# Loading both top-2 expert weights per visit instead of keeping all eight experts on chip

## The chip, the cores and the metric

The kernel runs on one core of one Trainium2 chip. The core has five engines that run side by side: TensorE (PE, matmuls), VectorE (DVE), ScalarE (ACT), GpSimd (POOL) and SyncE (SP, which here only issues DMAs). They meet only at semaphores. The metric is device time in microseconds (us), lower is better, given as the median of several runs.

## The reference

The input is `x`, 16 sequences of 256 tokens with 256 features. Four blocks are added to it one after the other: an mLSTM-like attention, an expert layer of 16 experts with fixed capacity, a causal linear attention, and a top-2 expert layer with a layer norm at its end. The change touches the last one. Cut to what matters (T = 4096 tokens, D = 256, H = 1024, E = 8):

```python
logits = x @ Wg + bg                          # T x 8
top2_vals, top2_idx = top_k(logits, 2)
scores = softmax(top2_vals)
h = gelu(x @ W1[e] + b1[e])                   # W1[e]: 256 x 1024
y = h @ W2[e] + b2[e]                         # W2[e]: 1024 x 256
out = sum over the two chosen e of scores * y
return layer_norm(x + out, gamma, beta)
```

Each expert has 1 MB of W1 and 1 MB of W2 in fp32, so the eight experts have 8 MB of each.

## The kernel before, in words

One program per engine runs through five stages; every order is written out by hand. Stage 1 is the first attention with the shared expert, stage 2 the 16 experts with fixed capacity, stage 3 the linear attention with the routing of the top-2 layer, stage 4 the top-2 experts, stage 5 the layer norm.

**Stage 4.** The 8192 pairs of token and expert are sorted by expert into slots in DRAM (`dSL`, written by stage 3). The stage makes 39 visits: 32 of 256 slots ("full") and 7 of 128 slots ("half", for experts whose slots cross a tile boundary; the half visits are number 8, 13, 18 and so on to 38). A table `te` on chip holds, for each visit, the expert and the first slot. A visit has four units of work for PE: two halves of W1 (`up`, L2013) and two halves of W2 (`down`, L2032). fp32 products are made of three fp32r products, so each half of a weight is split first: its high part `wh` by ACT (L2130; for the last unit of a visit by DVE, L2073) and its low part `wl` by DVE (L2077). Both go into rings of three. PE's order is the list `UNITS`: the last W2 half of a visit comes after the first W1 half of the next visit. ACT and DVE prepare a unit two units ahead of PE (`w_high(n + 2)`, `w_low(n + 2)`).

**Where the weights are.** `W1` (64 KB per partition) is filled by SP during stage 2 (L1388), one expert every second step; `W2` (64 KB per partition) during stage 3 (L1938), one expert per step. In stage 4, ACT and DVE each read the expert's number of a visit from `te` into a register (`value_load`, L2119 and L2064) before its first unit, and address the resident weights with it.

**What else runs in stage 4.** SP loads for each visit the slot entries `es` (`entries`, L2210) and the biases `b1c`, `b2c` (`biases`, L2216 and L2219), each behind a `value_load` of its own. POOL gathers the tokens of a visit (`xs`, L2178), three visits ahead, adds `beta` to the output (L2191), and scatters the results with addition into DRAM (`dOUT`, L2197). The scatter of a visit waits for that of the visit before (`sy_st`); the results lie in a ring of two. `entries(i)` waits for the scatter of visit i - 6. So SP is paced by the scatters.

**Start of stage 4.** SP waits until all slots are written, loads `es`, POOL gathers, PE transposes (L1994), ACT and DVE split the tokens, PE starts.

Of the kernel before, what the change touches and what calls it, by code (L numbers as in the profile page):

```python
# [10 lines left out]
ALU = mybir.AluOpType  # L11
# [76 lines left out]
def build(nc, A, out):  # L88
    ctx = ExitStack()
    with ctx:  # L90
        sigs = []

        def sig(name):
            s = Sig(ctx.enter_context(nc.semaphore(name)))
            sigs.append(s)
            return s

        def ring(name, n):
            return [sig(f"{name}{i}") for i in range(n)]
# [1051 lines left out]
        M3 = Mem()  # L1151
        W1 = M3.sb("W1", [128, E1, 2, H1])
        M2 = Mem()
# [15 lines left out]
        sc_st = ring("expert_y_added", 4)  # L1169
        w1_ld = sig("w1_loaded")  # L1170
        pe_ex, v_ex, a_ex = sig("pe_expert"), sig("dve_expert"), sig("act_expert")
# [201 lines left out]
        def sp_stage2(sp):  # L1373
            def w_load(x, m):
                expert_w_in(sp, x, m)

            w_load(1, 2)
            for x in range(E0):
                for f in range(2):
                    if x + 2 < E0:  # L1380
                        w_load(x + 2, f)
                if x == 5:
                    sp.wait_ge(*v_sl.of("empty"))
                    sp.dma_start(dSL.rearrange("(k p j) e -> p k (j e)", p=128, j=8),
                                 slz[:, :, :].rearrange("p j e -> p (j e)").unsqueeze(1).to_broadcast([128, SLROWS // 1024, 128])
                                 ).then_inc(*init_st.up("slots", by=16))
                if x % 2 == 0:
                    sp.dma_start(W1[:, x // 2, :, :], A["W1"][x // 2].rearrange("(k p) f -> p k f", p=128)).then_inc(*w1_ld.up(x, by=16))  # L1388
                if x + 2 < E0:
                    w_load(x + 2, 2)  # L1390
# [14 lines left out]
        M6 = Mem()  # L1405
        W2 = M6.sb("W2", [128, E1, 8, D])
# [3 lines left out]
        M4 = Mem()  # L1410
        firsts = M4.ring("firsts", 2, [128, 8, 5])
        before = M4.ring("before", 2, [128, 8, 5])
# [3 lines left out]
        mask3 = M4.sb("mask3", [128, 3, 128])  # L1416
        w1r = M4.sb("w1r", [128, 2, E1])
        bgr = M4.sb("bgr", [128, E1])
# [22 lines left out]
        ln_ld, beta_st = sig("final_w_loaded"), sig("beta_added")  # L1441
        r3_ld, w2_ld, init_st, pad_st = sig("top2_w_loaded"), sig("w2_loaded"), sig("slots_cleared"), sig("pads_cleared")
        sl_g, v_sl = sig("pool_empty_slots"), sig("dve_empty_slots")
# [27 lines left out]
        def pe_stage3(pe):  # L1471
# [36 lines left out]
            def logits(j):  # L1508
                was = banks[6].take(v_l1, "l", j)
                if was:  # L1510
                    pe.wait_ge(*was)
                if j == 0:
                    pe.wait_ge(*r3_ld.all())
                for c in range(4):
                    if c % 2 == 0:
                        pe.wait_ge(*a_l1.of("zT", 2 * j + c // 2))
                    for k in range(2):
                        ins = pe.matmul(banks[6].t[:, 8 * c:8 * c + 8], zT[j % 2][:, k, 128 * c:128 * c + 128], w1r[:, k, :], start=k == 0, stop=k == 1)
                ins.then_inc(*pe_l1.up("l", j))
# [271 lines left out]
        def act_stage3(a):  # L1791
            a.dma_start(w1r[:, :, :], A["L1g"].rearrange("(k p) e -> p k e", p=128)).then_inc(*r3_ld.up("w", by=16))
            a.dma_start(bgr[:, :], to_all(A["bg"], E1)).then_inc(*r3_ld.up("b", by=16))
# [106 lines left out]
        def sp_stage3(sp):  # L1900
# [10 lines left out]

            W2_AT = {x: (x,) for x in range(E1)}
            sp.wait_ge(*pe_ex.of("x", E0 - 1, 3))
# [12 lines left out]
            for i in STEPS:  # L1926
                if at(i) is not None:
                    sp.wait_ge(*v_l1.of("x3", 2 * i + 1))
                    sp.dma_start(by_chunk(out[pair_rows(i), :]), x2[i % 4][:, :, :]).then_inc(*x3_st[i % 4].up(i, by=16))
                    if i and at(i + 4) is not None:  # L1930
                        ctxT_in(i + 4)
                    sp.wait_ge(*a_l1.of("z", 2 * i + 1))
                    for d_ in (dZ, dOUT):
                        sp.dma_start(by_chunk(d_[pair_rows(i), :]), z3[i % 3][:, :, :]).then_inc(*z_st[i % 3].up(i, by=16))
                if at(i + 4) is not None:
                    x_in(i + 4)
                for x in W2_AT.get(i, ()):
                    sp.dma_start(W2[:, x, :, :], A["W2"][x].rearrange("(k p) f -> p k f", p=128)).then_inc(*w2_ld.up(x, by=16))  # L1938
            for s in (*x3_st, *z_st):
# [4 lines left out]

        M7 = Mem()
        xs = M7.ring("xs", 3, [128, 2, D])
        es = M7.ring("es", 6, [128, 2, 2])
# [9 lines left out]
        y1 = M7.ring("y1", 2, [128, 2, D])  # L1957
        w1f = W1[:, :, :, :].rearrange("p x k f -> p (x k) f")
        w2f = W2[:, :, :, :].rearrange("p x k f -> p (x k f)")
        es_ld, b1_ld = ring("tile_loaded", 6), ring("tile_b1_loaded", 6)  # L1960
        gz_ld = ring("tile_x_gathered", 3)
        b2_ld = ring("tile_b2_loaded", 4)
        sy_st = sig("tile_y_added")
        pe_t, v_t, a_t = sig("pe_tile"), sig("dve_tile"), sig("act_tile")
# [81 lines left out]
        def freed(n):  # L2046
            i, kind, half = UNITS[n]
            return ("up", i, half, 1) if kind == 1 else ("dn", i, half)

        def w_src(r, kind, half):  # L2050
            if kind == 1:
                return w1f[:, bass.ds(r * 2, 2), 512 * half:512 * half + 512]
            return w2f[:, bass.ds(r * 2048 + 1024 * half, 1024)]

# [4 lines left out]
        def dve_stage4(v):  # L2059
            regs = {}  # L2060

            def expert(i):
                if i not in regs:
                    regs[i] = v.value_load(te[0:1, 0, ORDER[i]:ORDER[i] + 1], min_val=0, max_val=E1 - 1)  # L2064
                    regs.pop(i - 2, None)
                return regs[i]

            def w_low(n):
                i, kind, half = UNITS[n]
                if n >= 3:  # L2070
                    v.wait_ge(*pe_t.of(*freed(n - 3)))
                if (kind, half) == (2, 1):
                    v.tensor_copy(w_dst(wh[n % 3], kind), w_src(expert(i), kind, half)).then_inc(*v_t.up("wh", n))  # L2073
                    v.wait_ge(*v_t.of("wh", n))
                else:
                    v.wait_ge(*a_t.of("w", n))
                v.tensor_tensor(w_dst(wl[n % 3], kind), w_src(expert(i), kind, half), w_dst(wh[n % 3], kind),  # L2077
                                ALU.subtract).then_inc(*v_t.up("w", n))

# [32 lines left out]
        def act_stage4(a):  # L2112
            regs = {}

            def expert(i):
                if i not in regs:
                    if i == FIRST:
                        a.wait_ge(*v_r3.of("part tiles"))
                    regs[i] = a.value_load(te[0:1, 0, ORDER[i]:ORDER[i] + 1], min_val=0, max_val=E1 - 1)  # L2119
                    regs.pop(i - 2, None)  # L2120
                return regs[i]

            def w_high(n):
                i, kind, half = UNITS[n]
                if (kind, half) != (2, 1):
                    if n == 2:
                        a.wait_ge(*w2_ld.all())
                    if n >= 3:
                        a.wait_ge(*pe_t.of(*freed(n - 3)))
                    a.copy(w_dst(wh[n % 3], kind), w_src(expert(i), kind, half)).then_inc(*a_t.up("w", n))  # L2130

# [5 lines left out]

            for s in (w1_ld, pad_st, *x3_st, *z_st):
                a.wait_ge(*s.all())
# [63 lines left out]
        def sp_stage4(sp):  # L2203
# [8 lines left out]
            def biases(i):  # L2212
# [6 lines left out]
                sp.dma_start(b2c[i % 4][:, :], A["b2"][bass.ds(r, 1), :].to_broadcast([128, D])).then_inc(*b2_ld[i % 4].up(i, by=16))  # L2219

            sp.wait_ge(*sx_st.all())
            sp.wait_ge(*v_r3.of("full tiles"))
            for i in range(VISITS + 2):
                if i < VISITS:
                    entries(i)
                if i >= 2:
                    biases(i - 2)
                if i == 5:
                    sp.dma_start(gam[:, :], to_all(A["gamma"], D)).then_inc(*ln_ld.up("g", by=16))
                    sp.dma_start(bet[:, :], to_all(A["beta"], D)).then_inc(*ln_ld.up("b", by=16))  # L2230
# [202 lines left out]
```

## Time and profile before

| what | value |
|---|---|
| median of 3 runs | 1310.1 us (1306.51 to 1312.15) |
| span of the profiled execution | 1302.7 us |
| PE busy | 1134.3 us (87%) |
| DVE, ACT, POOL busy | 71%, 62%, 50% |
| PE busy in stages 2, 3 and 4 | 99%, 70%, 98% |
| stage 4, from PE's first `up` to its last `down` | about 804 to 1256 us |
| DMA traffic | 166.83 MB, mean 128 GB/s |

The span runs from the first to the last instruction of one profiled execution, whose own run time is not recorded beside it; the three timed runs lie 3.8 to 9.4 us above that span. Times of instructions are taken from the span. "Granted clock" is the share of TensorE's full speed that the chip granted.

### The profile page before, as it was taken

To read this page: it belongs to the slowest core of one execution; us is meant where nothing else is said; L and a number is where in the kernel's file an instruction comes from. 1 tells how busy PE (TensorE), PEld (TensorE's weight loads), DVE (VectorE), ACT (ScalarE), POOL (GpSimd) and SP (SyncE) were. 2 spreads that over 40 slices of the span, in tenths; PEclk is the share of its full clock that TensorE was granted. 3 is DMA by queue.
4 is the path that set the end of the run, shared out by engine and by line. 5 is a ranking of instruction groups with operands and counts; after the bars stand their busy time and mean duration, and the time that the engine had idled before them with its cause. 6 is when DMAs were issued, how large, how long until landed. Compare 5 with 4: busy or idle time off the path is not lost.

```text
span 1302.7 us, 23898 instructions
## 1 busy us (share of the span) xinstructions
PE 1134.3 (87%) x8296; PEld 1042.6 (80%) x8296; DVE 919.8 (71%) x1964; ACT 804.1 (62%) x1611; POOL 657.6 (50%) x581
## 2 busy tenths in 40 slices
PE   4789999988879999999969953999999999999950
PEld 2678787877758888888868753999999999999950
DVE  5677888677656666666537755877878878787857
ACT  3656566653336565565537533787877777778846
POOL 2434442443255555666344774366566654445336
PEclk8668999999989999999988866999999999999985
DMA  6544332321345686777558972245454533333239
GB/s 203 200 147 150 135 138 107 105 71 46 122 146 149 162 236 183 195 190 191 112 126 285 294 226 60 42 64 79 73 83 67 86 54 56 54 55 58 46 86 241
DMA packets 148295, 166.83 MB, mean 128 GB/s; under 512 B 28528, under 2 KB 129008, under 8 KB 146128
## 3 DMA queue, kind: packets, MB, share of 16 engines
q1 hardware_dynamic: 112176, 122.02, 28.9%
q0 software_dynamic: 35040, 42.75, 20.2%
q8 instruction: 66, 1.08, 0.3%
q10 hardware_dynamic: 960, 0.54, 0.1%
q14 instruction: 53, 0.43, 0.1%
HBM read 114.74 MB, written 50.53 MB: 127 GB/s over the span
## 4 chain that ended last, share of the span: by engine, by line
PE 68%; DVE 13%; ACT 6%; issue 6%; POOL 5%; DMA 2%; ACTq 0%; SPq 0%; DVEq 0%; POOLq 0%
PE quad L2013 15%; PE pb L2032 13%; PE quad L1200 13%; PE pb L1215 7%; PE quad L298 4%; PE pb L352 4%; DVE Dm L527 2%; PE pb L366 2%; POOL dSL L1882 2%; ACT Dm L839 1%; PE quad L1994 1%; PE pb L264 1%; PE quad L1480 1%; PE pb L1185 1%; ACT gl L2159 1%
## 5 line engine op out<-in xcount | busy, mean ns | idle before, releaser
L2077 DVE TENSOR_TENSOR wl<-W,wh 128x1024 fp32r<-128x1024 f32 x156 | 188.3, 1228 | 78.0 <-ACT gl L2159 55.6
L2197 POOL DMA_INDIRECT dOUT<-y,es x71 | 134.8, 1898 | 198.6 <-DVE y L2109 185.9
L2032 PE MATMUL pb<-wh,hh 128*128 128x256 f32 x568 | 164.4, 289 | 0.5 <-DVE hl L2096 0.2
L2032 PE MATMUL pb<-wh,hl 128*128 128x256 f32 x568 | 160.6, 283 | 0.0
L2032 PE MATMUL pb<-wl,hh 128*128 128x256 f32 x568 | 160.6, 283 | 0.0
L1346 POOL DMA_INDIRECT dACC<-ye,idxJ x64 | 100.3, 1567 | 103.7 <-ACT ye L1310 54.7
L2159 ACT ACTIVATE gl<-quad,b1c 128x256 f32<-128x256 f32 (+1 forms) x312 | 124.7, 451 | 19.4 <-PE quad L2013 19.1
L2130 ACT CAST wh<-W 128x1024 fp32r x117 | 122.0, 1048 | 22.0 <-DVE Q L1766 8.2
L2013 PE MATMUL quad<-xh,wh 128*128 128x256 f32 (+1 forms) x624 | 125.5, 283 | 8.2 <-ACT hh L2164 6.7
L2013 PE MATMUL quad<-xl,wh 128*128 128x256 f32 (+1 forms) x624 | 125.4, 283 | 0.0
L2013 PE MATMUL quad<-xh,wl 128*128 128x256 f32 (+1 forms) x624 | 125.4, 283 | 0.0
L2032 PEld LDWEIGHTS pb<-wh,hh 128*128 128x128 f32 x568 | 108.8, 191 | 1.2 <-DVE wl L2077 0.6
L2032 PEld LDWEIGHTS pb<-wl,hh 128*128 128x128 f32 x568 | 108.9, 192 | 0.0
L2032 PEld LDWEIGHTS pb<-wh,hl 128*128 128x128 f32 x568 | 108.7, 191 | 0.0
L2096 DVE TENSOR_TENSOR hl<-gl,hh 128x512 fp32r<-128x512 f32 (+1 forms) x156 | 97.2, 640 | 12.4 <-ACT hh L2164 9.0
L2013 PEld LDWEIGHTS quad<-xh,wh 128*128 128x128 f32 x624 | 97.5, 193 | 9.6 <-ACT hh L2164 7.7
L1304 ACT CAST ehh<-egf 128x512 fp32r<-128x512 f32 x64 | 39.7, 620 | 101.0 <-DVE egf L1249 101.0
L2178 POOL DMA_INDIRECT xs<-dZ,es x71 | 86.8, 1222 | 26.2 <-issue 18.6
L2013 PEld LDWEIGHTS quad<-xl,wh 128*128 128x128 f32 x624 | 97.5, 193 | 0.0
L2013 PEld LDWEIGHTS quad<-xh,wl 128*128 128x128 f32 x624 | 97.5, 193 | 0.0
L2164 ACT CAST hh<-gl 128x512 fp32r<-128x512 f32 (+1 forms) x156 | 90.9, 583 | 4.9
L1200 PE MATMUL quad<-xeh,ewh 128*128 128x512 f32 x256 | 84.5, 411 | 1.6 <-DVE xel L1243 1.6
(288 smaller groups left out, 3165.2 us busy)
## 6 DMA issues: line engine op xcount, KB each, us to landing
MB<-dM SPq DMA_DIRECT2D x16, 1024.0 KB, 5.3
W<-in_W SPq DMA_DIRECT2D x16, 1024.0 KB, 9.5
wraw<-in_Wg SPq DMA_DIRECT2D x16, 512.0 KB, 6.5
wraw<-in_Wu SPq DMA_DIRECT2D x16, 512.0 KB, 7.9
wraw<-in_Wd SPq DMA_DIRECT2D x16, 512.0 KB, 5.3
b2c<-in_b SPq DMA_DIRECT2D x39, 128.0 KB, 3.3
xp<-in_x SPq DMA_DIRECT2D x16, 256.0 KB, 5.4
cT<-in_ctxT SPq DMA_DIRECT2D x16, 256.0 KB, 4.9
```

The lines of the kernel that those rows point to most:

```text
L1200: ins = pe.matmul(bank.t[:, :], a_[m][x % 2][:, 512 * k + 128 * f:512 * k + 128 * f + 128], b_[x % 2][:, k, :], start=n == 0, stop=n == 5)
L1215: ins = pe.matmul(bank[:, 0:256], a_[x % 2][:, f, 128 * tt:128 * tt + 128], b_[2][x % 2][:, 256 * f:256 * f + 256], start=n == 0, stop=n = ...
L1346: g.indirect_dma_start(out=dACC[:, :], out_offset=bass.IndirectOffsetOnAxis(ap=idxJ[:, tt, x:x + 1], axis=0), in_=ye[x % 2][:, tt, :], in_ ...
L2013: ins = pe.matmul(bank[:, TS * c:TS * c + width(i)], ww[:, k, fs], xx[i % 2][:, k, 0:width(i)], start=m == 0, stop=m == 5)
L2032: ins = pe.matmul(bank.t[:, 0:256], a_[s][:, c, 128 * tt:128 * tt + 128], b_[n % 3][:, 256 * c:256 * c + 256], start=half == 0 and m == 0, ...
L2077: v.tensor_tensor(w_dst(wl[n % 3], kind), w_src(expert(i), kind, half), w_dst(wh[n % 3], kind), ALU.subtract).then_inc(*v_t.up("w", n))
L2096: v.tensor_tensor(hl[hidden(i, half)][:, 2 * q_:2 * q_ + 2, w], gl[(2 * (2 * i + half) + q_) % 3][:, :, w], hh[hidden(i, half)][:, 2 * q_: ...
L2130: a.copy(w_dst(wh[n % 3], kind), w_src(expert(i), kind, half)).then_inc(*a_t.up("w", n))
L2159: ins = a.activation(g_[:, c, 0:width(i)], ab4.of(i, half, q_)[:, TS * c:TS * c + width(i)], ACT.Gelu, bias=b1c[i % 6][:, cc:cc + 1])
L2164: a.copy(hh[hidden(i, half)][:, 2 * q_:2 * q_ + 2, 0:width(i)], g_[:, :, 0:width(i)]).then_inc(*a_t.up("hh", i, half, q_))
L2178: g.indirect_dma_start(out=xs[i % 3][:, c, :], out_offset=None, in_=dZ[:, :], in_offset=bass.IndirectOffsetOnAxis(ap=es[i % 6][:, c, 1:2]. ...
L2197: g.indirect_dma_start(out=dOUT[:, :], out_offset=bass.IndirectOffsetOnAxis(ap=es[i % 6][:, tt, 1:2].bitcast(U32), axis=0), in_=y1[i % 2][ ...
```

## The change

`W1` and `W2` are no longer loaded in stages 2 and 3. SP loads both weights of a visit's expert during stage 4, 1 MB each, into two rings of three buffers (8 KB per partition each). Their layout in DRAM is changed on the host so that each partition's 8 KB are contiguous. ACT and DVE read from the ring's buffer at a fixed address and have no `value_load` any more; ACT waits for the load's semaphore before its copy, DVE before the one it makes itself. SP gets one more `value_load` and two more loads per visit. The first visit's weights are issued ahead of the wait for the slots. Two unused tensors (`room`, `gap`) keep the place of the old weights in stages 2 and 3.

```diff
-        W1 = M3.sb("W1", [128, E1, 2, H1])
+        w1r = M3.ring("w1r", 3, [128, 2, H1])
+        M3.sb("room", [128, 5, 2, H1])
...
-                if x % 2 == 0:
-                    sp.dma_start(W1[:, x // 2, :, :], A["W1"][x // 2].rearrange("(k p) f -> p k f", p=128)).then_inc(*w1_ld.up(x, by=16))
...
-                for x in W2_AT.get(i, ()):
-                    sp.dma_start(W2[:, x, :, :], A["W2"][x].rearrange("(k p) f -> p k f", p=128)).then_inc(*w2_ld.up(x, by=16))
...
+        w2r = M7.ring("w2r", 3, [128, 2048])
...
-        def w_src(r, kind, half):
+        def w_src(i, kind, half):
             if kind == 1:
-                return w1f[:, bass.ds(r * 2, 2), 512 * half:512 * half + 512]
-            return w2f[:, bass.ds(r * 2048 + 1024 * half, 1024)]
+                return w1r[i % 3][:, :, 512 * half:512 * half + 512]
+            return w2r[i % 3][:, 1024 * half:1024 * half + 1024]
...
                     if n >= 3:
                         a.wait_ge(*pe_t.of(*freed(n - 3)))
-                    a.copy(w_dst(wh[n % 3], kind), w_src(expert(i), kind, half)).then_inc(*a_t.up("w", n))
+                    a.wait_ge(*(w1_ld if kind == 1 else w2_ld)[i % 3].of(i))
+                    a.copy(w_dst(wh[n % 3], kind), w_src(i, kind, half)).then_inc(*a_t.up("w", n))
...
+            def weights(i):
+                if i == FIRST:
+                    sp.wait_ge(*v_r3.of("part tiles"))
+                r = sp.value_load(te[0:1, 0, ORDER[i]:ORDER[i] + 1], min_val=0, max_val=E1 - 1)
+                if i >= 3:
+                    sp.wait_ge(*v_t.of("w", UNIT[i - 3, 1, 1]))
+                sp.dma_start(w1r[i % 3][:, :, :], A["W1"][bass.ds(r, 1), :, :, :].rearrange("a p k f -> (a p) k f")).then_inc(*w1_ld[i % 3].up(i, by=16))
+                if i >= 3:
+                    sp.wait_ge(*v_t.of("w", UNIT[i - 3, 2, 1]))
+                sp.dma_start(w2r[i % 3][:, :], A["W2"][bass.ds(r, 1), :, :].rearrange("a p c -> (a p) c")).then_inc(*w2_ld[i % 3].up(i, by=16))
+
+            sp.wait_ge(*v_r3.of("full tiles"))
+            weights(0)
             sp.wait_ge(*sx_st.all())
-            sp.wait_ge(*v_r3.of("full tiles"))
-            for i in range(VISITS + 2):
+            for i in range(VISITS + 3):
+                if 3 < i:
+                    weights(i - 3)
                 if i < VISITS:
                     entries(i)
-                if i >= 2:
+                if 2 <= i < VISITS + 2:
                     biases(i - 2)
```

## Rows read from the trace of the kernel before

**Rows 1.** The page: span, and busy us of each engine.
```profile
span 1302.7 us, 23898 instructions
PE 1134.3 (87%) x8296; PEld 1042.6 (80%) x8296; DVE 919.8 (71%) x1964; ACT 804.1 (62%) x1611; POOL 657.6 (50%) x581
```
**Rows 2.** Windows by stage: length, busy by engine, granted clock, DMA share, GB/s.
```profile
383.00:665.00 282.00, 280.28 (x1646) 248.28 (x1647) 166.54 (x237) 162.03 (x295) 154.30 (x117) 0.99 0.65 170
...
701.00:792.00 91.00, 63.95 (x327) 56.23 (x325) 62.30 (x319) 41.33 (x85) 70.88 (x70) 0.71 0.78 248
...
804.00:1257.00 453.00, 445.12 (x3714) 443.14 (x3714) 360.29 (x497) 354.25 (x653) 236.22 (x151) 1.00 0.39 62
```
**Rows 3.** Timeline of POOL in stage 3: start, length, operation, idle before it.
```profile
700.85 1.06 POOL L1882 DMA_INDIRECT dSL<-en,po  x1 [5.73 <-DVE po L1673]
...
725.29 0.96 POOL L1882 DMA_INDIRECT dSL<-en,po  x1 [0.30 <-issue]
...
790.63 0.96 POOL L1882 DMA_INDIRECT dSL<-en,po  x1 [0.30 <-issue]
```
**Rows 4.** Window over four full visits.
```profile
830.00:878.00 48.00, 48.00 (x404) 48.00 (x404) 38.58 (x53) 38.53 (x70) 26.27 (x18) 1.00 0.38 63
```
**Rows 5.** Waits of PE, 815 to 1258 us: us in total, times, longest.
```profile
PE quad L2013 <- ACT hh L2164: 6.7, 6, 1.7
```
**Rows 6.** The chain that ended last, around one stall: start, length, what.
```profile
964.74 1.50 PE pb L2032 x12
...
967.95 3.11 PE quad L2013 x24
...
978.69 2.88 PE quad L2013 x24
```
**Rows 7.** Timelines of ACT and of DVE ahead of the same stall.
```profile
962.99 0.51 ACT L2169 ACTIVATE y<-y,es 128x256 f32<-128x256 f32 x1 [1.80 <-DVE y L2106]
964.36 1.05 ACT L2130 CAST wh<-W 128x1024 fp32r x1 [0.87 <-issue]
...
966.62 1.23 DVE L2077 TENSOR_TENSOR wl<-W,wh 128x1024 fp32r<-128x1024 f32 x1 [2.95 <-ACT hh L2164]
```
**Rows 8.** Timelines of SP, of ACT and of POOL: one turn of the pacing.
```profile
912.71 0.34 SPq L2210 DMA_DIRECT2D es<-dSL  x1
913.81 0.34 SPq L2216 DMA_DIRECT2D b1c<-in_b  x1
914.33 0.33 SPq L2219 DMA_DIRECT2D b2c<-in_b  x1
...
928.67 1.05 ACT L2130 CAST wh<-W 128x1024 fp32r x1
...
936.23 0.39 SPq L2210 DMA_DIRECT2D es<-dSL  x1
...
940.94 1.63 POOL L2197 DMA_INDIRECT dOUT<-y,es  x1 [4.85 <-DVE y L2109]
```
**Rows 9.** DMA issues of the whole run: KB each, median us to landing.
```profile
MB<-dM SPq DMA_DIRECT2D x16, 1024.0 KB, 5.3
...
dOUT<-y,es POOLq DMA_INDIRECT x71, 3.9
```
**Rows 10.** The same from 420 to 520 us.
```profile
W<-in_W SPq DMA_DIRECT2D x2, 1024.0 KB, 11.5
dACC<-ye,idxJ POOLq DMA_INDIRECT x24, 3.9
```
**Rows 11.** DMA from 415 to 433 us in 40 slices of 0.45 us.
```profile
GB/s 0 64 116 118 132 152 257 284 316 346 380 391 401 414 405 387 410 360 392 419 410 373 373 339 246 214 123 57 16 7 100 127 64 0 0 0 0 0 0 0
```
**Rows 12.** Waits, 370 to 660 us: PE on the first gathers of stage 2.
```profile
PE pb L1185 <- DMA xe<-dH,idxJ: 2.4, 1, 2.4
```
**Rows 13.** The chain at the start of stage 4.
```profile
790.63 2.11 DMA dSL<-en,po
```
**Rows 14.** Timeline of ACT: the first copy of visit 1's W1.
```profile
810.57 1.05 ACT L2130 CAST wh<-W 128x1024 fp32r x1
```

More of the change, by code:

```diff
@@ L1169, in build @@
         sc_st = ring("expert_y_added", 4)
-        w1_ld = sig("w1_loaded")
+        w1_ld = ring("tile_w1_loaded", 3)
         pe_ex, v_ex, a_ex = sig("pe_expert"), sig("dve_expert"), sig("act_expert")
@@ L1405, in build @@
         M6 = Mem()
-        W2 = M6.sb("W2", [128, E1, 8, D])
         te = M6.sb("te", [128, 2, VISITS], I32)
@@ L1410, in build @@
         M4 = Mem()
+        M4.sb("gap", [128, E1, 8, D])
         firsts = M4.ring("firsts", 2, [128, 8, 5])
@@ L1416, in build @@
         mask3 = M4.sb("mask3", [128, 3, 128])
-        w1r = M4.sb("w1r", [128, 2, E1])
+        l1g = M4.sb("l1g", [128, 2, E1])
         bgr = M4.sb("bgr", [128, E1])
@@ L1441, in build @@
         ln_ld, beta_st = sig("final_w_loaded"), sig("beta_added")
-        r3_ld, w2_ld, init_st, pad_st = sig("top2_w_loaded"), sig("w2_loaded"), sig("slots_cleared"), sig("pads_cleared")
+        r3_ld, init_st, pad_st = sig("top2_w_loaded"), sig("slots_cleared"), sig("pads_cleared")
         sl_g, v_sl = sig("pool_empty_slots"), sig("dve_empty_slots")
@@ L1517, in logits @@
                     for k in range(2):
-                        ins = pe.matmul(banks[6].t[:, 8 * c:8 * c + 8], zT[j % 2][:, k, 128 * c:128 * c + 128], w1r[:, k, :], start=k == 0, stop=k == 1)
+                        ins = pe.matmul(banks[6].t[:, 8 * c:8 * c + 8], zT[j % 2][:, k, 128 * c:128 * c + 128], l1g[:, k, :], start=k == 0, stop=k == 1)
                 ins.then_inc(*pe_l1.up("l", j))
@@ L1791, in act_stage3 @@
         def act_stage3(a):
-            a.dma_start(w1r[:, :, :], A["L1g"].rearrange("(k p) e -> p k e", p=128)).then_inc(*r3_ld.up("w", by=16))
+            a.dma_start(l1g[:, :, :], A["L1g"].rearrange("(k p) e -> p k e", p=128)).then_inc(*r3_ld.up("w", by=16))
             a.dma_start(bgr[:, :], to_all(A["bg"], E1)).then_inc(*r3_ld.up("b", by=16))
@@ L1910, in x_in @@
                 sp.dma_start(x2[j % 4][:, :, :], by_chunk(dACC[pair_rows(j), :])).then_inc(*x2_ld[j % 4].up(j, by=16))
-            W2_AT = {x: (x,) for x in range(E1)}
             sp.wait_ge(*pe_ex.of("x", E0 - 1, 3))
@@ L1957, in build @@
         y1 = M7.ring("y1", 2, [128, 2, D])
-        w1f = W1[:, :, :, :].rearrange("p x k f -> p (x k) f")
-        w2f = W2[:, :, :, :].rearrange("p x k f -> p (x k f)")
         es_ld, b1_ld = ring("tile_loaded", 6), ring("tile_b1_loaded", 6)
@@ L1962, in build @@
         b2_ld = ring("tile_b2_loaded", 4)
+        w2_ld = ring("tile_w2_loaded", 3)
         sy_st = sig("tile_y_added")
@@ L2059, in dve_stage4 @@
         def dve_stage4(v):
[L2060 to L2066, printed above, removed]
             def w_low(n):
@@ L2071, in w_low @@
                     v.wait_ge(*pe_t.of(*freed(n - 3)))
+                src = w_src(i, kind, half)
                 if (kind, half) == (2, 1):
-                    v.tensor_copy(w_dst(wh[n % 3], kind), w_src(expert(i), kind, half)).then_inc(*v_t.up("wh", n))
+                    v.wait_ge(*w2_ld[i % 3].of(i))
+                    v.tensor_copy(w_dst(wh[n % 3], kind), src).then_inc(*v_t.up("wh", n))
                     v.wait_ge(*v_t.of("wh", n))
@@ L2076, in w_low @@
                     v.wait_ge(*a_t.of("w", n))
-                v.tensor_tensor(w_dst(wl[n % 3], kind), w_src(expert(i), kind, half), w_dst(wh[n % 3], kind),
-                                ALU.subtract).then_inc(*v_t.up("w", n))
+                v.tensor_tensor(w_dst(wl[n % 3], kind), src, w_dst(wh[n % 3], kind), ALU.subtract).then_inc(*v_t.up("w", n))
             def x_low(i):
@@ L2112, in act_stage4 @@
         def act_stage4(a):
[L2113 to L2121, printed above, removed]
             def w_high(n):
@@ L2125, in w_high @@
                 if (kind, half) != (2, 1):
-                    if n == 2:
-                        a.wait_ge(*w2_ld.all())
                     if n >= 3:
                         a.wait_ge(*pe_t.of(*freed(n - 3)))
-                    a.copy(w_dst(wh[n % 3], kind), w_src(expert(i), kind, half)).then_inc(*a_t.up("w", n))
+                    a.wait_ge(*(w1_ld if kind == 1 else w2_ld)[i % 3].of(i))
+                    a.copy(w_dst(wh[n % 3], kind), w_src(i, kind, half)).then_inc(*a_t.up("w", n))
             def x_high(i):
@@ L2136, in x_high @@
                 a.copy(xh[i % 2][:, :, 0:width(i)], banks[0].t[:, :].rearrange("p (k t) -> p k t", k=2)[:, :, 0:width(i)]).then_inc(*a_t.up("xh", i))
-            for s in (w1_ld, pad_st, *x3_st, *z_st):
+            for s in (pad_st, *x3_st, *z_st):
                 a.wait_ge(*s.all())
@@ L2418 @@
         "L1g": i["L1_ffn_Wg"], "bg": i["L1_ffn_bg"],
-        "W1": i["L1_ffn_W1"], "b1": t(i["L1_ffn_b1"].reshape(E1, 8, 128)),
-        "W2": i["L1_ffn_W2"], "b2": i["L1_ffn_b2"],
+        "W1": i["L1_ffn_W1"].reshape(E1, 2, 128, H1).transpose(0, 2, 1, 3), "b1": t(i["L1_ffn_b1"].reshape(E1, 8, 128)),
+        "W2": i["L1_ffn_W2"].reshape(E1, 8, 128, D).transpose(0, 2, 1, 3).reshape(E1, 128, 8 * D), "b2": i["L1_ffn_b2"],
         "gamma": i["L1_ffn_gamma"], "beta": i["L1_ffn_beta"],
```

## The prediction

> **What bounds the kernel now.** I read the page first: PE is busy 87% of the span, DVE 71%, the others less [rows 1]. So the first question is where PE is *not* the bound. The windows by stage answer it [rows 2]. Stage 2 (383 to 665 us): PE busy 280.3 of 282.0 us. Stage 3 (701 to 792): PE 64 of 91 us, DVE 62, POOL 71. Stage 4 (804 to 1257): PE 445.1 of 453.0 us at full clock. Stages 2 and 4 are PE's, and what is to be had or lost in stage 4 lies in 7.9 us of idle PE, or in a new wait.
>
> The timeline of POOL shows what bounds stage 3. It issues 64 slot writes from 700.85 to 791.59 us, one every 1.27 us (0.96 plus 0.30 of issue), with eight short `rsqrt` operations between them [rows 3]: 64 x 1.27 + 8 x 1.2 = 91 us, which is the stage. The write at 725 us takes 0.96 us in the middle of heavy DMA traffic, and so does the one at 790 us, after it has ended. POOL does not feel the traffic.
>
> For stage 4 I looked for PE's idle time by kind of visit. Four full visits: busy 48.00 of 48.00 us [rows 4]. The list of waits has six stalls of 6.7 us in all, 1.7 at most [rows 5]; in the timeline one stands behind each half visit but the last, which ends the stage. Of the 7.9 us, 0.7 lie behind PE's last matmul (about 1256.3 us), so 7.2 us are idle within the stage.
>
> One stall in detail [rows 6, 7]. PE ends a half visit's `down` at 964.74 + 1.50 = 966.24 and starts the next `up` at 967.95: 1.71 us idle. The list names ACT's `hh` as releaser, but the start fits DVE's `wl`: 966.62 + 1.23 = 967.85. That `wl` waits for ACT's `wh` (964.36 to 965.41), yet starts 1.21 us after it. ACT's `wh` itself starts 0.86 us after `y` has ended (963.50), with no wait but "issue". In both gaps the code has a `value_load` of the expert's number and the address made from it. What one costs is seen on SP, where the next DMA comes 0.76 us after `es` with a `value_load` between (913.05 to 913.81) and 0.18 us after `b1c` without one [rows 8]: 0.58 us.
>
> **Stages 2 and 3 lose their loads.** Eight issues of SP and 8 MB of traffic go in each. In stage 2 the cover is PE (1.7 us idle in 282), so they are worth nothing there, with one exception at its start: PE waits 2.4 us for the first gathers [rows 12], while three expert weights and W1's first megabyte are in flight. Bounds 0 and -2.4 us; W1 is last in its queue, so I take -0.5. In stage 3 the cover is POOL's 91 us, unaffected by traffic [rows 3]: 0. If that cover were gone, the 8 MB would be worth 8.4 MB / 400 GB/s = 21 us of DMA time, the rate being that of a saturated stretch [rows 11].
>
> **Stage 4, the two `value_load`s.** In a full visit they hide behind PE: 0. At a half visit they are on the path: ACT `y`, `value_load`, `wh`, `value_load`, `wl`, PE. Without them I expect the gap on ACT to fall from 0.86 to about 0.2 us and that on DVE from 1.21 to about 0.3: 1.5 us earlier. The shorter stalls vanish, the one of 1.71 leaves 0.2, and the 0.5 us of idle time outside the six stalls stays: 7.2 - 0.7 = 6.5 us. At least one `value_load` per stall goes (6 x 0.58 = 3.5 us), at most all 7.2. After a stall, the first `up` takes 3.11 against 2.88 us [rows 6], 0.23 x 6 = 1.4 us; I take half, -0.7, bounds 0 and -1.4. Who is late next? PE, which then has no idle left.
>
> **Stage 4, the loads.** 39 x 2.10 MB = 81.8 MB over 453 us is 181 GB/s on top of 62 [rows 2], 243 GB/s: less than the 248 that stage 3 moved and well under the 400 of a saturated stretch [rows 2, 11]. Bandwidth suffices on the mean; the question is lateness. `weights(i)` comes in SP's program after the biases of two steps before, so it is paced by the scatter of visit i - 4. For visit 11: `es` at 912.71 (released by the scatter of visit 7), `b2c` ends at 914.66, one `value_load` more, W1 issued at about 915.4 us. ACT needs it for the `wh` after `y` of visit 9, at 928.67 [rows 8]. That leaves 13.3 us. A load of 1 MB lands in 5.3 us with little beside it and 11.5 us behind 1.5 MB of other weights [rows 9, 10]. Both are under 13.3: 0. W2 follows by 2.6 us at 400 GB/s and is needed two units later. The buffers are free by then (DVE has made `wl` of visit i - 3), so these waits hold up nobody. SP's own 1.8 us more per visit delay `es` and the biases, which are needed two and three visits later: 0.
>
> Other work that shares the DMA engines: the scatter of visit 9 has landed by about 935.5 (SP's `es` at 936.23 less its `value_load`), and that of visit 10 starts at 940.94 [rows 8], so a scatter can land over 5 us later before POOL waits. The same form of scatter landed in 3.9 us amid weight loads at up to 400 GB/s in stage 2, and in 3.9 us in the quiet stage 4 [rows 9 to 11]. So 0 is my value; the other end is that rival below.
>
> **Start of stage 4.** 2.1 MB are issued at about 784.5 us, when the table is ready and POOL has some five slot writes to go [rows 3], and need 5.2 us of transfer plus a start: done by about 792. The last slot write lands at 792.74 [rows 13], with `es` behind it, both on the path. They may be held up a little: +0.6, bounds 0 and +2.1 (one landing more). The second visit's W1 is issued around 802, behind the biases of visit 1, and needed at 810.6 [rows 14]: hidden at 5.3 us, 3 us late at 11.5, which would cost PE at most about 1.5. I take 0.
>
> **The sum.** -0.5 - 6.5 - 0.7 + 0.6 = -7.1 us, against the span of 1302.7: 1295.6. Carried to the median (1310.1, 7.4 us above that span): 1303.0 us. Bounds of the terms: best -2.4 - 7.2 - 1.4 = -11.0, 1299; worst -3.5 + 2.1 + 1.5 = +0.1, 1310.
>
> **Rivals.**
> *Half the gain.* The stall is made of other things than `value_load`: the half visit's short units leave DVE and ACT too little time, and the order of `y` behind `wl` on DVE remains. For it: the gaps on ACT and DVE are larger at the stall than one `value_load` of 0.58. Against: nothing else is between those instructions. It gives -3.5 + 0.6 = -2.9 or less: 1305 to 1310 us. Chance 0.25.
>
> *The reload loop closes (the slower one).* A load waits for a scatter, PE for the load, the scatter for PE, over two visits. It decides once scatter delay d plus W1's landing L exceeds 13.3 us; each us over costs half a us per visit, x 38. With L = 11.5 as in stage 2 and d = 5.2 (each of a visit's two blocks held up by half of an expert's load, 2 x 1.05 MB at 400 GB/s), it is 16.7, 3.4 over: 1.7 x 38 = 65 us, 1368 us. With L = 5.3 the same d gives 10.5: nothing. Against it: the two figures of 3.9 us, and L = 11.5 contains 3.9 us of other loads that stage 4 has not. The Trainium skill speaks for the delay ("DMA: Bandwidth & Descriptors", Queues, rings and completion order): an engine goes round between queues packet by packet, and a packet holds typically 9 to 17 descriptors, so that a small transfer stands behind a whole engine's share of a megabyte. By that rule the delay above would be the ordinary case; the 3.9 us of stage 2 do not show it, and no trace yet shows rows of 8 KB. Anything between no loss and that, a few stalls behind the half visits (where the 13.3 shrinks by some 3 us), costs 2 to 15 us. Chance of all this 0.15, a good half of it over 1316.7 us.
>
> *Traffic was in the way elsewhere.* Without 16 MB in stages 2 and 3 something off the list comes sooner, say all of the 2.4 us and 2 us of stage 3. 1297 to 1300 us. Chance 0.08.
>
> **How the numbers follow.** My forecast, 1300 to 1305 us, has 0.52; the rivals 0.25, 0.15, 0.08. A measurement tells about 0.5%, 6.6 us, from nothing: the border of "faster" is 1303.5, in the middle of the forecast. Faster: three fifths of 0.52 plus 0.08 and some of the half gain, 0.43. Slower, over 1316.7: 0.10. The rest, 0.47, is no change. The range takes the best bound less a little for the spread of runs (the three lie within 5.6 us), 1298, and reaches into the slow rival to 1313.
>
> **What the changed profile would show.** Right: PE idle for under 1 us between its first and last matmul of stage 4, which lie some 7 us closer together; no ACT or DVE gap above 0.4 us ahead of `wh` and `wl`, stage 3 still 91 us on POOL, stage 2 unchanged, about 240 GB/s in stage 4, `dOUT` landing under 9 us, W1 landing under 10. Wrong: ACT or DVE waiting on a DMA of `w1r` or `w2r`; POOL waiting on `dOUT`; stalls that stay with no `value_load` in them; a first `up` later than 804 us by more than 2.

## The result, and the profile after

| | before | after |
|---|---|---|
| median | 1309.67 us (1306.51 to 1312.15, 4 runs) | 1337.1 us (1327.45 to 1339.3, 4 runs) |
| ratio, 95% interval | | 1.0192 [1.0166, 1.0218] |
| profiled execution: span | 1302.7 us | 1337.6 us, its own time 1339.3 |

The change made the kernel 1.9% slower. I had forecast 1303.0 us, and the result lies outside the range of 1298 to 1313 as well. The time is 34 us above the forecast, and the sign was wrong.

The page of the changed kernel: the lines that answer to [rows 1], and the line with the shares of the chain that ended last:

```profile
span 1337.6 us, 23839 instructions
PE 1151.9 (86%) x8296; PEld 1056.3 (79%) x8296; DVE 920.9 (69%) x1964; ACT 801.4 (60%) x1611; POOL 649.2 (49%) x581
...
PE 56%; DMA 12%; DVE 12%; ACT 7%; issue 7%; POOL 4%; SPq 2%; ACTq 0%; DVEq 0%; POOLq 0%
```

No engine's share of the span has grown. PE's busy time has, by 17.6 us for the same 8296 matmuls: 11 us of it lie in stage 1 (experiment 1), 7 in stage 4. I read the stages next. The windows of the changed kernel, with the columns of [rows 2] (length, PE, PEld, DVE, ACT, POOL, granted clock, DMA share, GB/s); the stage-4 window is shifted to where the stage now lies:

```profile
383.00:665.00 282.00, 276.35 (x1596) 243.44 (x1597) 166.78 (x235) 160.97 (x293) 155.46 (x120) 0.99 0.60 148
...
812.50:1291.00 478.50, 451.97 (x3714) 447.34 (x3714) 363.37 (x497) 351.45 (x654) 227.93 (x151) 0.98 0.77 225
830.00:878.00 48.00, 48.00 (x404) 48.00 (x403) 39.27 (x53) 38.05 (x68) 24.49 (x17) 1.00 0.69 203
```

Over the same four full visits as in [rows 4] PE still has no gap: the extra 140 GB/s do not slow PE by themselves. In the stage as a whole 26.5 us of PE are idle, where [rows 2] had 7.9, and the same 3714 matmuls take 452.0 us, where they took 445.1. Part of these 7 us is the clock: windows of 1 us show it granted at 0.50, the lower of its two levels (1.2 GHz instead of 2.4), from about 932.9 to 936.3 us, behind a stall of 3.15 us, and from about 1178.7 to 1185.5 us, in and behind one of 4.76 us. In the first trace of the kernel before it is never that low between 816 and 1256 us.

The four parts of the span add up:

| part | before | after | difference |
|---|---|---|---|
| start to the first gather of stage 2 | 365.9 | 374.3 | +8.4 |
| from there to stage 4's first transpose | 435.4 (to 801.3) | 435.8 (to 810.1) | +0.4 |
| from there to the start of the last `down` | 454.6 (to 1255.9) | 479.9 (to 1290.0) | +25.3 |
| from there to the end | 46.8 | 47.6 | +0.8 |
| sum | 1302.7 | 1337.6 | +34.9 |

The 8.4 us lie ahead of everything that the change touches, and the first experiment below shows that they are not its doing: the kernel before varies by as much. The change's own loss lies in the third line. (When I speak of "stage 4" in us below, it is this third line, from first transpose to last `down`.)

The waits of the changed kernel from 815 to 1300 us (us in total, times, longest), all engines, and PE's own from 815 to 1292, which answer to [rows 5]:

```profile
POOL dOUT L2175 <- DMA dOUT<-y,es: 60.0, 11, 8.7
...
ACT wh L2108 <- DMA w1r<-in_W: 39.9, 12, 7.0
```
```profile
PE quad L2009 <- ACT hh L2142: 21.5, 11, 4.8
PE pb L2028 <- DVE wl L2067: 4.1, 9, 0.5
```

Two of the signs that I had named as "wrong" are there: ACT waits for `w1r`, and POOL waits for its own scatter `dOUT`. The DMA issues from 830 to 1250 us (KB each, median us to landing) say how late each of them is:

```profile
w1r<-in_W SPq DMA_DIRECT2D x34, 1024.0 KB, 6.6
w2r<-in_W SPq DMA_DIRECT2D x33, 1024.0 KB, 9.7
...
dOUT<-y,es POOLq DMA_INDIRECT x62, 8.1
xs<-dZ,es POOLq DMA_INDIRECT x62, 7.3
```

In the kernel before the scatters landed in 3.9 us [rows 9] and the gathers of `xs` in 3.0. W1 itself is not slow: 6.6 us, well inside the 13.3 that I had counted as slack. What is slow is the small traffic beside it.

The chain that ended last shows how the two combine. The changed kernel, 1120 to 1182 us (start, length, what):

```profile
1121.14 6.05 DMA w1r<-in_W
...
1154.37 1.31 PE quad L2009 x12
...
1156.46 10.48 DMA dOUT<-y,es
1166.95 0.28 SPq L2187
...
1168.00 0.40 SPq L2188
...
1169.69 0.33 SPq L2197
...
1170.78 7.86 DMA w1r<-in_W
1178.75 0.10 issue
...
1181.19 0.98 PE quad L2009 x3
```

Read it from top to bottom. A scatter issued at 1156.46 lands 10.48 us later. Only then may SP run L2187, the `entries` of visit i, which wait for the scatter of visit i-6 because they reuse its buffer. Behind them, in SP's program, stand the biases and then the weights of visit i-2. W1 leaves at 1170.78, takes 7.86 us, and ACT's copy, which had waited 6.95 us, starts at 1178.71. PE then makes the results that the next scatter waits for. Over the window from 830 to 1290 us, `dOUT` holds 18.5% of this chain and `w1r` 11.2%. That is the rival *The reload loop closes*.

In one place two scatters follow each other on the same chain, because POOL waits for the first before it issues the second:

```profile
958.59 10.07 DMA dOUT<-y,es
...
972.13 9.56 DMA dOUT<-y,es
```

The first lands at 968.66, the second is issued at 972.13 and releases SP at 981.70, and W1 leaves at 986.22. There the lateness of a scatter counts twice.

### The profile page after: what moved, and what is told of

Its sections match the earlier page's. It is cut to its first block, busy times and chain, and to the rows that moved or that the text cites. A ratio compares the mean times of both kernels' runs of the same rounds, so it can differ in the third digit from the quotient of the medians.

```text
span 1337.6 us, 23839 instructions
## 1 busy us (share of the span) xinstructions
PE 1151.9 (86%) x8296; PEld 1056.3 (79%) x8296; DVE 920.9 (69%) x1964; ACT 801.4 (60%) x1611; POOL 649.2 (49%) x581
## 4 chain that ended last, share of the span: by engine, by line
PE 56%; DMA 12%; DVE 12%; ACT 7%; issue 7%; POOL 4%; SPq 2%; ACTq 0%; DVEq 0%; POOLq 0%
PE quad L1201 13%; PE quad L2009 9%; PE pb L2028 8%; PE pb L1216 7%; DMA dOUT<-y,es 7%; PE quad L298 4%; PE pb L352 4%; DMA w1r<-in_W 4%; PE pb L366 2%; POOL dSL L1881 2%; ACT gl L2137 2%; DVE Dm L527 1%; PE pb L264 1%; ACT Dm L839 1%; PE quad L1479 1%
## 5 line engine op out<-in xcount | busy, mean ns | idle before, releaser
L2175 POOL DMA_INDIRECT dOUT<-y,es x71 | 128.1, 1804 | 232.7 <-DVE y L2098 104.8
L2067 DVE TENSOR_TENSOR wl<-w1r,wh 128x1024 fp32r<-128x1024 f32 x78 | 95.5, 1225 | 64.5 <-ACT wh L2108 52.3
L2009 PEld LDWEIGHTS quad<-xh,wh 128*128 128x128 f32 x624 | 99.2, 196 | 25.3 <-ACT hh L2142 23.4
L2108 ACT CAST wh<-w1r 128x1024 fp32r<-128x1024 f32 x78 | 81.2, 1042 | 60.9 <-DMA w1r<-in_W 53.2
L2067 DVE TENSOR_TENSOR wl<-w2r,wh 128x1024 fp32r<-128x1024 f32 x78 | 95.6, 1225 | 8.7 <-ACT wh L2108 7.4
```

The source lines that it names most:

```text
L2009: ins = pe.matmul(bank[:, TS * c:TS * c + width(i)], ww[:, k, fs], xx[i % 2][:, k, 0:width(i)], start=m == 0, stop=m == 5)
L2067: v.tensor_tensor(w_dst(wl[n % 3], kind), src, w_dst(wh[n % 3], kind), ALU.subtract).then_inc(*v_t.up("w", n))
L2108: a.copy(w_dst(wh[n % 3], kind), w_src(i, kind, half)).then_inc(*a_t.up("w", n))
L2175: g.indirect_dma_start(out=dOUT[:, :], out_offset=bass.IndirectOffsetOnAxis(ap=es[i % 6][:, tt, 1:2].bitcast(U32), axis=0), in_=y1[i % 2][ ...
```

## The experiments

Each comparison is with the kernel before, run on the same chip. The first four ran on one chip (before: 1311.17 us there), the next four on a second (1321.51 us), the last three on a third (1308.95 us). Across chips I compare ratios and the length of stage 4, not whole times. The traces of the second chip have no landing times for the scatters, the gathers or the weights in the middle of stage 4.

### 1. The kernel before, once more

No edit. It gives a second trace of before and the size of what varies on its own.

> The kernel before once more, profiled. All theories: 1307 to 1312 us, ratio 1.00 within 0.3%. What it tells: in the profile of the changed kernel stage 2's first gather came 8.4 us later than before (374.3 against 365.9 us), in a stage that the change doesn't touch. If that is the granted clock's own play in stage 1, this execution shows another value than 365.9 too, or its runs are spread by as much; if the 8.4 us belong to the changed kernel, it shows 366 again.

Measured: 1311.65 us (1305.51 to 1313.99), ratio 1.0006 [0.9986, 1.0026]. In this trace stage 2's first gather is issued at 373.4 us instead of 365.9, and stage 4 takes 455.9 us (454.6 before). The changed kernel's 374.3 is the same as this, so the 8.4 us of the table above are variation of stage 1, not an effect. The granted clock goes with it: up to the first gather PE is busy for 306.6 us at a mean of 0.91 in the first trace, for 318.1 us at 0.87 in this one, and for 317.7 us at 0.86 in the changed kernel. The change costs 479.9 - 455 = 25 us in stage 4.

### 2. Small loads: the edit without its traffic

```diff
+                k1, f1 = (2, H1) if i < 3 else (1, 256)
-                sp.dma_start(w1r[i % 3][:, :, :], ...
+                sp.dma_start(w1r[i % 3][:, 0:k1, 0:f1], ...
...
+                c1 = 2048 if i < 3 else 256
-                sp.dma_start(w2r[i % 3][:, :], ...
+                sp.dma_start(w2r[i % 3][:, 0:c1], ...
```

> The changed kernel, but from visit 3 on each weight load brings only 128 KB of its 1 MB (the visit computes with old weights for the rest); every wait, semaphore and register load stays. Theory A (the reload loop: full loads double the landing of the scatters, and scatter, load, copy and PE then close a ring over two visits) and theory B (the scatters alone, each waiting for the one before, become the bound): no traffic, so scatters land in 4 to 5 us, no wait on w1r, stage 4's stalls behind the half visits are gone with the register loads, 1300 to 1305 us. Theory C (it is the order of the waits, the new places of the tiles or the longer program of SP, not the traffic): 1330 us or more, with ACT waiting on w1r.

Measured: 1302.91 us, ratio 0.9941 [0.9918, 0.9964]. Stage 4 takes 445.7 us. No wait of ACT for `w1r`, and one of PE of 0.3 us from 815 us on. DMA issues of this run, 830 to 1250 us:

```profile
w1r<-in_W SPq DMA_DIRECT2D x35, 128.0 KB, 2.5
w2r<-in_W SPq DMA_DIRECT2D x35, 128.0 KB, 2.8
...
dOUT<-y,es POOLq DMA_INDIRECT x68, 3.9
```

With the same instructions, semaphores and order, and an eighth of the bytes, the scatter is back at 3.9 us and the kernel is 0.6% faster than before. So the loss is 479.9 - 445.7 = 34 us of traffic, against which the edit gives back some 9 to 10.

### 3. The kernel before with the expert known ahead

```diff
-                    regs[i] = v.value_load(te[0:1, 0, ORDER[i]:ORDER[i] + 1], min_val=0, max_val=E1 - 1)
+                    regs[i] = i % E1
```

(the same on ACT)

> The kernel before with the two register loads of the expert's number on ACT and DVE taken out: the visit computes with expert (visit modulo 8) at a fixed address instead of its own. Weights stay resident. My prediction's term: 6.5 us of stalls and 0.7 of restarts go, 1302 to 1304 us, PE idle under 1 us within stage 4. Rival (half the gain, the stalls are made of the half visits' short units): 1305 to 1309 us, with stalls left behind the half visits.

Measured: 1304.16 us, ratio 0.9945 [0.9921, 0.9968]; stage 4 445.9 us. PE's waits of 6.7 us at the half visits [rows 5] are gone; from 815 to 1255 us one of 0.3 us is left. This is the whole of what the edit can give: 9 to 10 us (454.6 or 455.9 less 445.9).

### 4. The weights one step earlier in SP's order

```diff
-                if 3 < i:
-                    weights(i - 3)
+                if 3 <= i < VISITS + 2:
+                    weights(i - 2)
```

> The changed kernel with weights(i - 2) in place of weights(i - 3) at each step of SP, so that a load is issued one visit earlier and is paced by the scatter one visit further back. The bytes are the same, scatters should land in 8 to 11 us still. Theory A: 12 us more slack for W1, so ACT waits for w1r under 5 us in all and the time falls to 1303 to 1315 us (POOL's own waits for scatters hide behind the ring of results). Theory B: the time stays at 1325 to 1340 us, with DVE waiting for scatters before y.

Measured: 1304.93 us, ratio 0.9969 [0.9947, 0.9992]; stage 4 446.4 us. The bytes are all there, the scatters are still slow (6.1 us, though not the 8 to 11 expected), W1 lands in 6.9 us, and neither ACT nor PE waits for it. The loss was thus not bandwidth: with the load in another place of SP's program it does not arise.

### 5 and 6. Only one of the two loads whole

The edit of experiment 2 for W2 alone, and for W1 alone.

> The changed kernel, with W1's loads whole and W2's cut to 128 KB from visit 3 on (the rest of W2 is that of older visits). Theory A says that the ring closes when the scatter's delay d plus W1's landing L is more than some 13 us, less behind half visits. Here L stays near 5.5 us, and d should halve with the bytes (scatters at 6 us instead of 8 to 10): the sum falls to 8, ACT waits for w1r under 3 us in all, 1301 to 1306 us. If instead W1's landing alone is what is late, the waits on w1r stay above 20 us in all and the time above 1320 us.

> The mirror: W2's loads whole, W1's cut to 128 KB from visit 3 on. L falls to 2.5 to 3 us, d as in the run before. Theory A: 1301 to 1306 us again. If the scatters' delay alone were the cause, whichever megabyte makes it, this and the run before would both stay at 1320 us or more.

Measured: small W2 1318.36 us, ratio 0.9974 [0.9942, 1.0006], stage 4 445.4 us; small W1 1318.26 us, ratio 0.9990 [0.9961, 1.0019], stage 4 446.5 us. Either megabyte alone leaves PE without a wait over 0.3 us in stage 4, and ACT waits 2.4 us for W1 with small W2, not at all with small W1 (from 840 us on): it takes both to close the loop. That the scatters' delay halved, as expected, can't be read in these traces; POOL waited for a scatter only once in each, for 3 us at the end of the stage. The changed kernel itself was not run on this chip; elsewhere it took 479.9 us for stage 4 in its first run and 474.4 in experiment 9. The times of 1301 to 1306 us were not met: this chip is slower with every kernel, and the ratios are yet 0.3 to 0.5% above the 0.9941 of both small. The reason is the start of the stage. On this chip stage 3 ran longer in every kernel (from the first gather of stage 2 to the first transpose 445.1 us even in experiment 8, the kernel before with one edit, against 435), and SP issued the first visit's weights right ahead of the first entries. The chain of the run with small W2 (start, length, what):

```profile
811.71 5.66 DMA es<-dSL
819.44 7.01 DMA xs<-dZ,es
```

and that of the changed kernel on its own chip:

```profile
802.65 1.66 DMA es<-dSL
806.38 3.56 DMA xs<-dZ,es
```

The 2 KB of entries and the first gather are held up by 4.0 and 3.5 us, 7.5 us together or 0.6%, when the 2 MB of weights leave 1.2 us ahead of them (810.55 for W2, 811.71 for the entries), and by nothing when they leave 8.4 us ahead (794.23 and 802.65).

### 7. Short rows

The weights in DRAM as they are in the inputs: W1's rows are 4 KB and W2's 1 KB, where the change's layout has 8 KB.

```diff
-                sp.dma_start(w2r[i % 3][:, :], A["W2"][bass.ds(r, 1), :, :].rearrange("a p c -> (a p) c"))
+                sp.dma_start(w2r[i % 3][:, :].rearrange("p (k d) -> p k d", k=8), A["W2"][bass.ds(r, 1), :, :].rearrange("a (k p) d -> p (a k) d", p=128))
```

(W1 likewise)

> The changed kernel with the weights in their first layout in DRAM: same bytes and issues, but W1 comes in rows of 4 KB and W2 in rows of 1 KB instead of 8 KB in one piece. If a scatter's row of 1 KB stands behind long pieces of the other queue (the packet theory), shorter ones let it through earlier: scatters at 5 to 7 us, and the time falls to 1305 to 1325 us. If it is the bytes in flight that count, scatters stay at 8 to 10 us, W2 lands later than before, and the time is 1335 us or more.

Measured: 1320.42 us, ratio 1.0009 [0.9974, 1.0045]; stage 4 450.5 us, with the slow start of experiments 5 and 6 on top. ACT still waits for W1, but in short pieces:

```profile
ACT wh L2108 <- DMA w1r<-in_W: 12.2, 10, 2.5
```

The loop is only just closed: 5 us of stage 4 are lost instead of 34 (first run of the changed kernel) or 29 (experiment 9). As the changed kernel was not run on this chip, that shorter rows ease the loop is likely and not shown. Why they would, this run does not settle: the four scatters among the longest pieces of its chain still take 7.5 to 9.1 us.

### 8. The register loads moved in the kernel before

All `value_load`s stay, but ACT and DVE read visit i+1's expert behind unit (2, 0) of visit i, away from the stall.

```diff
+                if (kind, half) == (2, 0) and i + 1 < VISITS:
+                    expert(i + 1)
```

> The kernel before, weights resident, output in full: ACT and DVE read the expert's number of the next visit behind the unit before the last of a visit, so that the register is there when it is needed. All theories that put the stalls down to the register loads: what the kernel without them gave, stage 4 shorter by 8 to 10 us, 1301 to 1305 us. If the address made from a register costs as much as the register's load, half of that, 1306 to 1308 us.

Measured: 1312.62 us, ratio 0.9936 [0.9909, 0.9963]; stage 4 447.3 us, no stall of PE at a half visit. (The time itself is above the expected 1301 to 1305 us, but the kernel before takes 1321.5 us on this chip.) What cost 8 to 9 us was not that the register is read, but that it is read between `y` and `wh`. Two lines on each of two engines in the old kernel give all that the change gives at its best, without its 82 MB.

### 9. The changed kernel, once more

No edit, on a third chip.

> The changed kernel, unchanged, beside the kernels below on one chip. Theory (the reload loop closes: a scatter that is late under the weight loads holds back SP's next entries, behind which the next weights are queued): ratio to the kernel before 1.015 to 1.025, stage 4 from its first transpose to its last `down` about 480 us against 455, scatters at 7 to 9 us. Rival (the loss of the first run belonged to that chip's state): ratio under 1.01.

Measured: 1339.85 us (1332.87 to 1341.73), ratio 1.0242 [1.0209, 1.0275]; stage 4 474.4 us; ACT waits 36.0 us for `w1r`, scatters land in 7.6 us (830 to 1250 us). The ratio of the first run was 1.0192 [1.0166, 1.0218]. The loss is the kernel's.

### 10. Eight buffers for the entries: the loop cut at its one link

```diff
-        es = M7.ring("es", 6, [128, 2, 2])
+        es = M7.ring("es", 8, [128, 2, 2])
...
-                if i >= 6:
-                    sp.wait_ge(*sy_st.of(i - 6))
+                if i >= 8:
+                    sp.wait_ge(*sy_st.of(i - 8))
```

(and `i % 8` wherever `es` or its semaphore is used)

> The changed kernel with eight buffers for the entries (es) in place of six, so that SP's load of the entries of visit i waits for the scatter of visit i-8 and not i-6; the weights stay where they are in SP's order, as large, and wait for their buffers as before. Theory (the loop closes through this wait): the scatters stay slow (6 to 8 us) and the loss goes all the same: W1 is issued up to 3 us sooner, ACT's waits on W1 fall from 40 us to under 5, stage 4 takes 446 to 450 us, ratio 0.993 to 0.999. Rival (the loads are late by themselves, because three buffers do not cover a W1 that lands in 7 to 8 us beside the slow scatters): ACT goes on waiting 20 us or more for W1, stage 4 over 465 us, ratio over 1.008. Third (POOL's own wait for the scatter before it carries the delay, through the gathers of xs): PE waits for xs, stage 4 over 460 us.

Measured: 1300.33 us (1297.79 to 1304.53), ratio 0.9947 [0.9927, 0.9966]; stage 4 445.4 us. DMA issues, 830 to 1250 us:

```profile
w2r<-in_W SPq DMA_DIRECT2D x35, 1024.0 KB, 7.4
w1r<-in_W SPq DMA_DIRECT2D x34, 1024.0 KB, 6.1
...
dOUT<-y,es POOLq DMA_INDIRECT x69, 7.0
```

The scatters are as good as unchanged (7.0 us against 7.6 in experiment 9), the bytes and SP's order are the same, and the 29 us are gone. POOL still waits 12.4 us for its own scatters (61.0 in experiment 9), but PE waits for nothing beyond 0.3 us, so the third theory falls too. SP's waits from 815 to 1292 us name what changed. In the changed kernel:

```profile
SPq L2187 <- DMA dOUT<-y,es: 270.2, 32, 11.8
SPq L2208 <- DVE wl L2067: 10.1, 3, 4.8
```

With eight buffers:

```profile
SPq L2208 <- DVE wl L2067: 152.3, 36, 4.9
SPq L2197 <- DVE y L2095: 94.0, 35, 4.6
...
SPq L2187 <- DMA dOUT<-y,es: 3.7, 13, 0.4
```

SP was paced by scatters; now it is paced by DVE, that is, by the buffers coming free. That also pulls the two loads of a visit apart, as the timeline of SP shows. First the changed kernel, then the one with eight buffers (start, length, instruction):

```profile
1157.26 0.34 SPq L2205 DMA_DIRECT2D w1r<-in_W  x1
1157.72 0.37 SPq L2208 DMA_DIRECT2D w2r<-in_W  x1
1168.00 0.40 SPq L2188 DMA_DIRECT2D es<-dSL  x1
```
```profile
1101.15 0.34 SPq L2205 DMA_DIRECT2D w1r<-in_W  x1
1106.43 0.33 SPq L2208 DMA_DIRECT2D w2r<-in_W  x1
```

When SP is late, both buffers have long been free, and 2 MB leave within 0.46 us. When it is on time, W2 leaves 5.3 us behind W1. The window over stage 4 with eight buffers:

```profile
807.50:1252.00 444.50, 442.91 (x3714) 442.56 (x3714) 364.86 (x497) 353.49 (x655) 230.13 (x152) 0.99 0.87 243
```

PE is idle for 1.6 us, at 243 GB/s, which is the rate that I had worked out. So bandwidth does suffice, as the prediction says.

### 11. Short rows and the earlier step together

The edits of experiments 4 and 7.

> The changed kernel with both of its repairs: W1 and W2 in the layout that they have in the inputs (rows of 4 KB and of 1 KB in place of 8 KB), and the weights one step earlier in SP's order. Theory: no wait for W1 is left with the earlier step alone, so that shorter rows add nothing: stage 4 445 to 449 us, ratio 0.993 to 0.998, as with the earlier step alone (0.9969). Rival (longer rows hold up the scatters and gathers in places that the earlier step did not mend): ratio 0.990 to 0.993, scatters under 5 us. Against both: the many short rows load the DMA engines more (busy share over 0.8), stage 4 over 450 us, ratio 0.998 to 1.003.

Measured: 1304.27 us, ratio 0.9955 [0.9935, 0.9975]; stage 4 446.7 us; scatters 5.9 us. With the loads in time the length of the rows is worth nothing that these runs show: 0.9955 against 0.9969 for the earlier step alone is within the intervals, and the scatters land hardly sooner (5.9 against 6.1 us; at most 8.4 against 10.4).

## Why the prediction was wrong

**The step that failed** is the term at 0 for the loads of stage 4, and in it the scatter's delay d: "The same form of scatter landed in 3.9 us amid weight loads at up to 400 GB/s in stage 2, and in 3.9 us in the quiet stage 4 [rows 9 to 11]. So 0 is my value". The runs showed 34 us in its place (479.9 us of stage 4 against 445.7 with small loads). The 3.9 us are a median over the 24 scatters of a hundred microseconds (3.7 us at least, 7.5 at most), and the loads of that stretch come in bursts with gaps. Most of the scatters landed as fast as without loads. Asked for the inside of one burst alone, the trace of the kernel before (DMA issues from 419 to 424 us, a stretch at 392 GB/s) says:

```profile
dACC<-ye,idxJ POOLq DMA_INDIRECT x2, 6.3
xe<-dH,idxJ POOLq DMA_INDIRECT x1, 7.1
```

6.3 us for two scatters, 2.4 more than the median. I had also allowed a scatter to be 5 us late before POOL waits; on the chain it was 6.6 us late, and POOL waited 11 times. The number of the burst was there to be read; I had put the rate of the burst beside the landing of the stretch. With it d is not 0 but 2 to 3 us as the least value. That alone would not have closed the loop either, by my own condition: 2.4 + 6.6 = 9.0 us, under 10.3. The full loads of stage 4 held the scatters up by more than that burst did.

**The rule beside it pointed the right way.** The Trainium skill ("DMA: Bandwidth & Descriptors", Queues, rings and completion order) has an engine go round between its queues packet by packet. From that I had worked out that a small transfer stands behind shares of a large one, and had let the 3.9 us outweigh it. This case's traces agree with the direction: scatters land in 3.9 us beside loads of 128 KB, and in 7.0 to 8.1 us beside the full ones with rows of 8 KB (6.1 in experiment 4). They do not show that the length of a packet sets the delay. By that rule W2's packets would be an eighth as long with rows of 1 KB instead of 8 KB. The scatters still took 5.9 us, against 6.1 with the long rows (experiments 11 and 4). My estimate of the delay, d = 5.2 us, worked out from the bytes and the rate of [rows 11], lies between the median excess (8.1 - 3.9 = 4.2) and that of the scatter on the chain (10.48 - 3.9 = 6.6).

**The loop's condition was about right, and left something out.** I had written that it decides once d + L exceeds 13.3 us, and some 3 us sooner behind a half visit. By the medians, 4.2 + 6.6 = 10.8: under 13.3, at the edge of 10.3. In the window shown, 6.6 + 7.9 = 14.5: over. So it closed in places, the six stretches around the half visits, and not in each visit as my 65 us assumed: 34 us, between "2 to 15" and 65. Two things were not in the condition. Where POOL waits for the scatter before, the lateness of two scatters adds up, as the chain shows at 958.59 and 972.13 us. And once SP is late, W1 and W2 leave together. That this makes the next scatters later still is argued and fits the medians (8.1 and 7.6 us in the changed kernel, 7.0 where the two are apart); how many of the 34 us are due to it no run separates. Besides, 34 us are not all idle time: the matmuls take 452.0 us in the changed kernel's stage and 442.9 in experiment 10's, some 9 of the 34 us, with the spells of lower clock and the slow matmuls behind stalls in them. Experiments 4 and 10 show the mechanism by opening it at two different links with the traffic kept; experiment 2 by taking the traffic away.

**The register loads: right in mechanism, too small in size.** I had -6.5 for the stalls and -0.7 for the slow matmuls behind them, -7.2; experiments 2, 3 and 10 show -9 to -10. The stalls went entirely, as said. The idle time was sized well: PE's idle time in the stage's window falls from 7.9 us [rows 2], or 8.4 in experiment 1's trace, to 1.6. The window of that trace:

```profile
811.00:1266.00 455.00, 446.56 (x3714) 444.79 (x3714) 360.27 (x497) 355.47 (x655) 236.48 (x152) 0.99 0.39 62
```

The rest is in the matmuls: with stalls they take 445.1 us [rows 2] and 446.6, without them 442.9 (experiment 10) and 443.4 (experiment 3, 811 to 1256 us). That is 2 to 4 us where I had 0.7 with a bound of 1.4. One restart of 3.11 against 2.88 us [rows 6] was not all that a stall can cost behind it: in experiment 1's trace the clock was granted at 0.50 from about 976.3 to 979.7 us, behind a stall of 1.76 us. Behind the stall of 1.71 us in [rows 6] it was not. *Half the gain* falls with experiments 3 and 8.

**Stages 2 and 3: right.** 435.4 and 435.8 us with and without the loads, and 433.8 to 436.2 in the four traces of the first chip. *Traffic was in the way elsewhere* falls.

**Start of stage 4: right on one chip, too small on another.** I had +0.6 with a bound of +2.1. Experiment 5 shows +7.5 us where the weights leave right ahead of the entries, and in experiments 6 and 7 `es` and `xs` land as late (5.9 and 7.1 us, 6.0 and 6.0 us). My bound counted one landing held up; there are two in a row, `es` and then `xs`. What makes stage 3 longer on that chip stays open.

**W2: right.** It lands in 9.7 us and no wait of ACT or DVE for it stands in the list.

## What to carry to other kernels

When a change puts large loads beside small transfers on which an order depends, read how long the small ones take inside a burst, not their median over the stage, and follow that delay round: what waits for the small transfer, and what is queued behind the waiting instruction. If the large loads themselves are queued there, the loop can feed itself, and a cheap cut (two more buffers of 16 bytes per partition, or the load one step earlier) is worth more than any saving of bytes. Before moving 82 MB to be rid of a register load, move the register load: the kernel before with its `value_load`s one unit earlier (0.9936) and the changed kernel with eight entry buffers (0.9947) beat both kernels, by 0.5 to 0.6% over the kernel before, and their intervals do not tell them apart.

## What the runs showed of the hardware

- Slow small transfers cost nothing here as long as nothing in order waits for them: with eight buffers the scatters take 7.0 us instead of 3.9, the DMA engines are 87% busy, and PE idles for 1.6 us in 444.5.
- The 2 KB entries, queued by SP just behind 2 MB, took 5.7 to 6.0 us (experiments 5 to 7) instead of 1.7 to 1.8 (the changed kernel, the kernel before).
- The length of stage 1 varies in the same kernel: the first gather of stage 2 was issued at 365.9 or at 373.4 us in two traces of the kernel before. With it goes the mean granted clock of the whole span, 0.924 or 0.911. A difference of 8 us between two single traces means nothing until it is read stage by stage.
- A stall of PE can cost more than its idle time. The granted clock fell to 0.50 for 3.4 to 6.8 us at stalls of 1.76, 3.15 and 4.76 us, and stayed at 1.00 behind one of 1.71 us.
